# Head softmax on six single score banks, with a later inverse product and the last addition on VectorE

## The chip, the core and the metric

One core of a Trainium2 chip runs the whole kernel. The metric is device microseconds from start to end, as the median of several runs; less is better.

## What is computed

The kernel is a four-layer decoder on a stream of 2 x 512 tokens with 256 features and a context of 2 x 1024 tokens. The change touches one of its attentions, the cross attention of layer 1, whose softmax runs over the 16 heads and not over the keys:

```python
scores = jnp.einsum('bhqd,bhkd->bhqk', mh_q, mh_k) / sqrt(HD)   # 16 heads of 16 features
score = jax.nn.softmax(scores, axis=1)                          # axis 1: the heads
att = jnp.einsum('bhqk,bhkd->bhqd', score, mh_v)
```

So for each pair of a query and a key there is one maximum and one sum over 16 numbers, and nothing is carried from key to key but the product with the values.

## The kernel before

`head_softmax_stage` (tiles named `a1x_...`) computes this attention in 64 tiles: 2 batches, 4 query tiles and 8 key tiles, each of 128 keys (partitions) by 128 queries by 16 heads. The order on every engine is written out by hand, with semaphores between the engines; each engine takes its instructions in order. Tile n goes through these steps:

- **Scores** (TensorE, `score`, L1471): 16 products of 128 columns into `scores`, a ring of three double banks of 8 heads each; a tile fills two. Each half waits until the exponentials have read what stood there three halves before.
- **Maximum** (VectorE, L1530): one reduction over 2048 numbers, where the tile's two double banks lie next to each other. In every third tile they wrap around the ring; then two reductions of 1024 (L1534) go into `most_half`, and a small maximum of the two (L1536) joins them.
- **Shift** (TensorE, `shift`, L1482): four products of 512 columns subtract the maximum from the scores in place.
- **Exponential** (ScalarE, L1551): two of 1024 columns, into one of four buffers of `experts`.
- **Sum over heads** (GpSimd): four additions, of 1024 (L1588), 512 (L1590), 256 (L1592) and 128 columns (L1596, into `total`).
- **Inverse** (ScalarE, `invert`, L1559 and L1564): the logarithm, and the exponential of its negative, into a PSUM bank.
- **Division** (VectorE, `divide`, L1520): one product over 2048 columns, in place.
- **Value product** (TensorE, `value`, L1497): 32 instructions that add over eight key tiles into `u`, which `u_out` on ScalarE (L1570) copies out after the eighth.

The engines interleave tiles. VectorE takes the maximum of tile n and then the division of tile n-2. TensorE takes the first half of the scores of n+1, the shift of n, the second half of the scores of n+1, and the values of n-2. ScalarE takes the exponentials of n and then the inverse of n-1. SyncE loads the second batch's queries, keys and values piece by piece, each piece after a wait on the count of scores or value products that frees its place.

Of the kernel before, what the change touches and what calls it, by code (L numbers as in the profile page):

```python
# [17 lines left out]
P = 128  # L18
# [1356 lines left out]
def head_softmax_stage(core, name, qs, ks, q_parts, k_parts, v_scr, aoT, ex, loads=()):  # L1375
# [12 lines left out]
    HALVES = 2  # L1388
    with stage(core, name) as st:
# [12 lines left out]
        mh = st.sb("most_half", [P, HALVES, P])  # L1402
        tree = st.sb("tree", [P, 8, P])
        tree2 = st.sb("tree2", [P, 4, P])
        tree3 = st.sb("tree3", [P, 2, P])
# [11 lines left out]
        with nc.Block() as block:  # L1417
            @block.sync
            def _(sp):
                def load(b, which, part):  # L1420
                    for dst, src in head_softmax_loads(qs, ks, b, which, part, q_parts, k_parts):
                        sp.dma_start(dst, src).then_inc((q_in, k_in)[which][part], 16)

                def load_values(b, t):
                    sp.dma_start(vs[:, t, :], v_scr[b, t * P:(t + 1) * P].rearrange("t g c -> t (g c)")
                                 ).then_inc(v_in[t], 16)

                load(0, 1, 1)
                core.landed(sp)
                for t in range(4):  # L1430
                    load_values(0, t)
                load(0, 1, 2)
                for t in range(4, 6):
                    load_values(0, t)
                load(0, 1, 3)
                for t in range(6, KT):
                    load_values(0, t)
                load(0, 0, 1)
                prefetch(sp, loads, loaded)
                for b in range(1, B):  # L1440

                    sp.wait_ge(scored, HALVES * (b * UB - 2 * KT))
                    load(b, 0, 0)
                    for quarter in range(4):

                        sp.wait_ge(scored, HALVES * (b * UB - KT + 2 * quarter + 2))
                        load(b, 1, quarter)
                        for t in range(2 * quarter, 2 * quarter + 2):
                            sp.wait_ge(valued, b * UB - KT + t + 1)
                            load_values(b, t)  # L1450
                    load(b, 0, 1)
                end_prefetch(sp, loads, loaded)

            @block.tensor
            def _(pe):
                def score(n, half):
                    b, qt, kt = place(n)
                    if n == 0 and half == 0:
                        pe.wait_ge(core.first_in, core.first_at)
                    if half == 0 and kt == 0 and qt % (QT // 2) == 0 and (b or qt):  # L1460
                        pe.wait_ge(q_in[2 * qt // QT], (b + (qt > 0)) * (16 * len(RUNS)))
                    if half == 0 and qt == 0 and kt % 2 == 0 and (b or kt):
                        pe.wait_ge(k_in[kt // 2], (b + (kt > 0)) * (16 * len(RUNS)))
                    g = HALVES * n + half
                    if g >= 3:

                        pe.wait_ge(expd, g - 2)
                    for i in range(2):
                        for j in range(4):
                            h = 8 * half + 4 * i + j  # L1470
                            mm = nc.tensor.matmul(sp_[:, g % 3, i, j, :], ks[0:96, h, kt * P:(kt + 1) * P],  # L1471
                                                  qs[0:96, h, qt * P:(qt + 1) * P], start=(j == 0), stop=False,
                                                  skip_group_check=True)
                    mm.then_inc(scored, 1)

                def shift(n):

                    pe.wait_ge(most, n + 1)
                    for half in range(HALVES):
                        g = HALVES * n + half  # L1480
                        for i in range(2):
                            mm = nc.tensor.matmul(sp_[:, g % 3, i, :, :], minus[:, :],  # L1482
                                                  mx[:, n % 2, :].unsqueeze(1).to_broadcast([P, 4, P]),
                                                  start=False, stop=True, skip_group_check=True)
                        mm.then_inc(less, 1)
# [17 lines left out]
                for half in range(HALVES):  # L1503
                    score(0, half)
# [12 lines left out]
            def _(dve):  # L1517
# [6 lines left out]
                nc.vector.tensor_scalar(minus[:, :], core.ident_bf[:, :], -1.0, None, ALU.mult).then_inc(minus_in, 1)  # L1524
                for n in range(N):
                    dve.wait_ge(scored, HALVES * (n + 1))
                    g = HALVES * n % 3
                    if g < 2:
                        src = sp_[:, g:g + 2, :, :, :].rearrange("p g i j q -> p q (g i j)")
                        nc.vector.tensor_reduce(mx[:, n % 2, :], src, AX.X, ALU.max).then_inc(most, 1)  # L1530
                    else:
                        for half in range(HALVES):
                            src = sp_[:, (g + half) % 3, :, :, :].rearrange("p i j q -> p q (i j)")
                            nc.vector.tensor_reduce(mh[:, half, :], src, AX.X, ALU.max).then_inc(most_half, 1)  # L1534
                        dve.wait_ge(most_half, HALVES * (n // 3 + 1))
                        nc.vector.tensor_tensor(mx[:, n % 2, :], mh[:, 0, :], mh[:, 1, :], ALU.max).then_inc(most, 1)  # L1536
                    if n >= 2:
                        divide(n - 2)
# [4 lines left out]
            def _(act):  # L1543
                def exp(n):
# [3 lines left out]
                    for half in range(HALVES):  # L1548
                        g = HALVES * n + half
                        act.wait_ge(less, g + 1)  # L1550
                        nc.scalar.activation(ex[:, n % E, 8 * half:8 * half + 8, :],  # L1551
                                             sp_[:, g % 3, :, :, :].rearrange("p i j q -> p (i j) q"), ACT.Exp
# [31 lines left out]
            def _(pool):  # L1584
                for n in range(N):
                    e = ex[:, n % E, :, :]
                    pool.wait_ge(expd, HALVES * (n + 1))
# [2405 lines left out]
```

## Time and profile before

| | |
|---|---|
| time, median of 3 runs | 2276.43 us (2266.73 to 2276.82) |
| span of the profiled execution | 2262.2 us; its own time, which is not listed apart, is one of this kind: the runs lie 4.5 to 14.6 us above this span |
| busy over the whole span | TensorE 81%, VectorE 65%, ScalarE 47%, GpSimd 36% |
| the stage | first score at 704.6 us, end of the last copy at 1052.8 us |

The span runs from the first to the last instruction. An engine's busy time is what the profiler records of its instructions; bracketed in a row of the timeline stands how long the engine sat idle before an instruction, and what released it. Most of the kernel lies outside the stage and is the same before and after the change.

### The profile page before, as it was taken

Reading aid. Unit: us, or ns where it says so; the run is one execution under the profiler, and the core shown is the slowest. Engines: PE = TensorE matmul, PEld = TensorE weight load, DVE = VectorE, ACT = ScalarE, POOL = GpSimd, SP = SyncE. Lnnn points to the kernel's source line nnn. Section 1 sums busy time; section 2 is a strip of 40 time slices with the busy share of each in tenths; the row PEclk is TensorE's granted clock in tenths of the full one; section 3 lists DMA queues with packets and bytes.
Section 4 is the critical chain, followed back from the end, with each engine's and each line's share of the span. In section 5 each row is a group of like instructions: output and inputs, shape, how many; then the busy total and the mean of one; then the engine's idle time right before and its main releaser. Section 6 shows DMA issues by size and latency. Waiting matters only on the chain. (4 is left out here: it accounts for less than half of the span.)

```text
span 2262.2 us, 32189 instructions
## 1 busy us (share of the span) xinstructions
PE 1835.8 (81%) x11356; PEld 920.9 (41%) x11379; DVE 1477.1 (65%) x2550; ACT 1073.0 (47%) x1821; POOL 823.1 (36%) x744
## 2 busy tenths in 40 slices
PE   5888979999875767767797788999879796899954
PEld 3444423333543444445485452333246543122223
DVE  4544266663666998896434547999744555788676
ACT  3453124445333444453344343888834424266746
POOL 1000035554244999995304110666732222000012
PEclk9999989999986898898797899999979897699967
DMA  6612551210029115001514844222035500444000
GB/s 187 161 37 84 190 169 63 66 47 1 19 71 223 24 21 94 2 1 71 190 41 142 190 136 97 69 54 65 20 134 194 166 10 17 104 106 93 20 1 19
DMA packets 174401, 192.08 MB, mean 85 GB/s; under 512 B 15844, under 2 KB 140334, under 8 KB 173334
## 3 DMA queue, kind: packets, MB, share of 16 engines
q1 hardware_dynamic: 171172, 181.64, 29.5%
q0 software_dynamic: 3072, 8.39, 1.2%
q8 instruction: 93, 1.52, 0.3%
q14 instruction: 64, 0.52, 0.1%
HBM read 125.61 MB, written 68.30 MB: 86 GB/s over the span
## 5 line engine op out<-in xcount | busy, mean ns | idle before, releaser
L3461 POOL TENSOR_TENSOR a2x_masked<-a2x_masked,tall_rows 128x512 f32<-128x512 f32 x128 | 163.2, 1276 | 126.3 <-ACT a2x_masked L3423 126.3
L1551 ACT ACTIVATE experts<-a1x_scores 128x1024 f32<-128x1024 f32 x128 | 124.1, 1021 | 163.7 <-PE a1x_scores L1482 163.7
L3472 DVE TENSOR_REDUCE a3x_row_most<-a3x_ring 128x1 f32<-128x512 f32 x256 | 162.9, 684 | 26.0 <-PE a3x_ring L3311 24.9
L3472 DVE TENSOR_REDUCE a2x_row_most<-a2x_ring 128x1 f32<-128x512 f32 x256 | 162.3, 679 | 5.0 <-DMA a2a_qs<-a2a_shift 3.4
L1588 POOL TENSOR_TENSOR a1x_tree<-experts 128x1024 f32<-128x1024 f32 x64 | 150.4, 2350 | 32.9 <-ACT experts L1551 32.4
L671 POOL TENSOR_TENSOR a0x_pair_sums<-a0x_probs_T 128x1024 f32<-128x1024 f32 x48 | 114.8, 2391 | 129.2 <-ACT a0x_probs_T L800 101.8
L854 DVE TENSOR_REDUCE ctx_then_heads<-a0x_rows 128x2 f32<-128x1024 f32 x88 | 107.7, 1224 | 81.7 <-PE a0x_rows L689 81.5
L1520 DVE TENSOR_TENSOR experts<-experts,a1x_inverse_total 128x2048 f32<-128x2048 f32 x64 | 145.7, 2276 | 4.2 <-ACT a1x_inverse_total L1564 4.2
L3416 ACT ACTIVATE a3x_probs_T<-a3x_scores_T 128x1024 f32<-128x1024 f32 x128 | 123.0, 1018 | 46.6 <-PE a3x_scores_T L3338 46.6
L1471 PE MATMUL a1x_scores<-a1x_qs,a1x_ks 96*128 96x128 bf16 x1024 | 93.0, 244 | 59.3 <-ACT experts L1551 45.0
L3416 ACT ACTIVATE wide_rows<-a2x_masked 128x1024 f32<-128x1024 f32 x128 | 135.9, 1062 | 1.4 <-POOL a2x_masked L3461 1.4
L800 ACT ACTIVATE a0x_probs_T<-a0x_scores_T 128x1024 f32<-128x1024 f32 x96 | 98.3, 1024 | 76.6 <-PE a0x_scores_T L715 63.6
L1530 DVE TENSOR_REDUCE a1x_most<-a1x_scores 128x128 bf16<-128x2048 f32 x43 | 98.5, 2291 | 33.2 <-PE a1x_scores L1471 33.2
L1482 PE MATMUL a1x_scores<-a1x_most,a1x_minus_ident 128*128 128x512 bf16 x256 | 71.6, 405 | 56.7 <-DVE a1x_most L1536 32.5
L1471 PEld LDWEIGHTS a1x_scores<-a1x_qs,a1x_ks 96*128 96x128 bf16 x1024 | 69.1, 110 | 108.5 <-ACT experts L1551 78.5
L3311 PE MATMUL a2x_ring<-a2x_ks,a2x_qs 97*128 97x512 bf16 x256 | 99.2, 387 | 8.2 <-DMA a2x_qs<-in_ones_bf 5.2
L3484 DVE TENSOR_TENSOR a2x_masked<-a2x_scores_T,tall_rows 128x512 f32<-128x512 f32 x128 | 87.6, 685 | 22.7 <-ACT wide_rows L3416 13.8
L711 PE MATMUL a0x_scores_T<-ctx_then_heads 64*128 64x512 f32 x384 | 101.6, 607 | 0.7 <-ACT ctx_then_heads L806 0.7
L728 PE MATMUL a0x_u<-a0x_probs_T,a0x_vs 128*64 128x512 f32 x384 | 92.8, 605 | 0.0
L3423 ACT COPY a2x_masked<-a2x_scores_T 128x512 f32<-128x512 f32 x128 | 74.7, 584 | 36.7 <-PE a2x_scores_T L3338 30.5
L1497 PE MATMUL a1x_u<-experts,a1x_vs 128*32 128x128 f32 x2048 | 86.3, 321 | 6.1 <-DVE experts L1520 6.1
L3314 PE MATMUL a2x_ring<-wide_rows,ident_bf 128*128 128x512 bf16 x234 | 90.1, 385 | 0.0
(676 smaller groups left out, 4206.0 us busy)
## 6 DMA issues: line engine op xcount, KB each, us to landing
v_scr<-p0x_vout SPq DMA_DIRECT2D x24, 256.0 KB, 2.0
k_scr<-p0x_x SPq DMA_DIRECT2D x24, 256.0 KB, 2.3
ctx_then_heads<-k_scr SPq DMA_DIRECT2D x8, 768.0 KB
a0x_vs<-v_scr SPq DMA_DIRECT2D x8, 768.0 KB, 4.8
experts<-in_L_ffn_w SPq DMA_DIRECT2D x8, 768.0 KB, 6.7
v_scr<-experts SPq DMA_DIRECT2D x16, 256.0 KB, 2.2
a1x_vs<-v_scr SPq DMA_DIRECT2D x16, 256.0 KB, 5.5
v_scr<-m1f_vout SPq DMA_DIRECT2D x16, 256.0 KB, 2.5
```

The costliest lines, as they stand in the source:

```text
L671: nc.gpsimd.tensor_tensor(pair[:, n // 2 % RP, :, :], pT[:, (n - 1) % R, :, :], pT[:, n % R, :, :], ALU.add).then_inc(paired, 1)
L711: nc.tensor.matmul(sT[:, n % 2, h, :], ks[hs, u % 3, kt * P:(kt + 1) * P], qs[hs, u % 3, :], start=True, stop=False, skip_group_check=True)
L854: nc.vector.tensor_reduce(rm[:, qt, :, c], row_psum(r)[:, :, :], AX.X, ALU.max).then_inc(row_most, 1)
L1471: mm = nc.tensor.matmul(sp_[:, g % 3, i, j, :], ks[0:96, h, kt * P:(kt + 1) * P], qs[0:96, h, qt * P:(qt + 1) * P], start=(j == 0), stop=F ...
L1520: nc.vector.tensor_tensor(ex[:, n % E, :, :], ex[:, n % E, :, :], rp[:, 0, :].unsqueeze(1).to_broadcast([P, H, P]), ALU.mult).then_inc(nor ...
L1530: nc.vector.tensor_reduce(mx[:, n % 2, :], src, AX.X, ALU.max).then_inc(most, 1)
L1551: nc.scalar.activation(ex[:, n % E, 8 * half:8 * half + 8, :], sp_[:, g % 3, :, :, :].rearrange("p i j q -> p (i j) q"), ACT.Exp).then_inc ...
L1588: nc.gpsimd.tensor_tensor(tree[:, :, :], e[:, 0:8], e[:, 8:16], ALU.add).then_inc(folded, 1)
L3311: mm = nc.tensor.matmul(out, lhsT, rhs, start=True, stop=True, skip_group_check=True)
L3416: nc.scalar.activation(pT[:, n % R, 2 * half:2 * half + 2, 0:w], src, ACT.Exp).then_inc(expd, 1)
L3461: nc.gpsimd.tensor_tensor(sm[:, i % 2, 1, :], sm[:, i % 2, 1, :], full[1][:, i // 2 % KT, :], ALU.add).then_inc(pool_masked, 1)
L3472: nc.vector.tensor_reduce(rm[:, u % 2, h * QT + qt:h * QT + qt + 1, part], ring[:, row_place(r) % 3, 0:n], AX.X, ALU.max).then_inc(row_mos ...
```

## The change

The ring of three double banks becomes a ring of six single banks of four heads. Scores, shift and exponentials count banks: four waits and signals a tile where there were two, and four exponentials of 512 columns where there were two of 1024. A bank of new scores waits for the exponential of that bank alone. On VectorE the division comes three tiles behind the maximum and not two; on ScalarE the inverse comes two tiles behind the exponentials and not one; on TensorE the value product comes four tiles behind, and stands ahead of the shift. In the third tile that wraps, the two half reductions each wait for their own two banks. The last of the four additions of the sum over heads (128 columns, into `total`) moves from GpSimd to VectorE, between the maximum and the division; `tree3` gets a second buffer for it.

```diff
-    HALVES = 2
+    BANKS = 4
+    RING = 6
...
-        sp_ = st.ps("scores", [P, 3, 2, 4, P])
+        sp_ = st.ps("scores", [P, RING, 4, P])
...
-                    sp.wait_ge(scored, HALVES * (b * UB - 2 * KT))
+                    sp.wait_ge(scored, BANKS * (b * UB - 2 * KT))
...
+                    g = BANKS * n + i
+                    if g >= RING:
+
+                        pe.wait_ge(expd, g - RING + 1)
+                    for j in range(4):
...
                 for n in range(N):
                     if n + 1 < N:
                         score(n + 1, 0)
+                        score(n + 1, 1)
+                    if n >= 4:
+                        value(n - 4)
                     shift(n)
                     if n + 1 < N:
-                        score(n + 1, 1)
-                    if n >= 2:
-                        value(n - 2)
-                value(N - 2)
-                value(N - 1)
+                        score(n + 1, 2)
+                        score(n + 1, 3)
+                for n in range(N - 4, N):
+                    value(n)
...
+                def most_of(n):
+                    at = BANKS * n % RING
+                    if at + BANKS <= RING:
+                        dve.wait_ge(scored, BANKS * (n + 1))
+                        src = sp_[:, at:at + BANKS, :, :].rearrange("p i j q -> p q (i j)")
+                        nc.vector.tensor_reduce(mx[:, n % 2, :], src, AX.X, ALU.max).then_inc(most, 1)
+                        return
+                    for half, i in enumerate((at, 0)):
+                        dve.wait_ge(scored, BANKS * n + 2 * half + 2)
+                        src = sp_[:, i:i + 2, :, :].rearrange("p i j q -> p q (i j)")
+                        nc.vector.tensor_reduce(mh[:, half, :], src, AX.X, ALU.max).then_inc(most_half, 1)
+                    dve.wait_ge(most_half, 2 * (n // 3 + 1))
+                    nc.vector.tensor_tensor(mx[:, n % 2, :], mh[:, 0, :], mh[:, 1, :], ALU.max).then_inc(most, 1)
+
+                def add_up(n):
+                    dve.wait_ge(folded, 3 * (n + 1))
+                    if n >= 2:
+                        dve.wait_ge(logged, n - 1)
+                    nc.vector.tensor_tensor(tot[:, n % 2], tree3[:, n % 2, 0], tree3[:, n % 2, 1], ALU.add
+                                            ).then_inc(total, 1)
+
                 for n in range(N):
...
+                    most_of(n)
                     if n >= 2:
-                        divide(n - 2)
+                        add_up(n - 2)
+                    if n >= 3:
+                        divide(n - 3)
+                add_up(N - 2)
+                divide(N - 3)
+                add_up(N - 1)
                 divide(N - 2)
                 divide(N - 1)
...
                 for n in range(N):
+                    if n >= KT and n % KT == 3:
+                        u_out(n - 4)
                     exp(n)
-                    if n >= 1:
-                        invert(n - 1)
-                    if n >= KT and n % KT == 1:
-                        u_out(n - 2)
+                    if n >= 2:
+                        invert(n - 2)
+                invert(N - 2)
                 invert(N - 1)
                 u_out(N - 1)
...
-                    nc.gpsimd.tensor_tensor(tree3[:, :, :], tree2[:, 0:2], tree2[:, 2:4], ALU.add).then_inc(folded, 1)
-                    pool.wait_ge(folded, n * 3 + 3)
                     if n >= 2:
-                        pool.wait_ge(logged, n - 1)
-                    nc.gpsimd.tensor_tensor(tot[:, n % 2], tree3[:, 0], tree3[:, 1], ALU.add).then_inc(total, 1)
+                        pool.wait_ge(total, n - 1)
+                    nc.gpsimd.tensor_tensor(tree3[:, n % 2], tree2[:, 0:2], tree2[:, 2:4], ALU.add).then_inc(folded, 1)
```

## Rows read from the trace of the kernel before

**Rows 1.** Windows view, steady stretch: busy us of PE, PEld, DVE, ACT, POOL

```profile
712.00:1040.00 328.00, 228.14 (x3198) 145.57 (x3196) 294.23 (x167) 157.04 (x256) 299.79 (x250) 0.88 0.22 38
```

**Rows 2.** Groups by line, same stretch: busy us, mean ns, idle us before

```profile
L1588 POOL TENSOR_TENSOR a1x_tree<-experts 128x1024 f32<-128x1024 f32 x63 | 148.0, 2350 | 32.9 <-ACT experts L1551 32.4
...
L1520 DVE TENSOR_TENSOR experts<-experts,a1x_inverse_total 128x2048 f32<-128x2048 f32 x62 | 141.1, 2276 | 0.0
...
L1590 POOL TENSOR_TENSOR a1x_tree<-a1x_tree 128x512 f32<-128x512 f32 x63 | 80.3, 1274 | 4.9
...
L1592 POOL TENSOR_TENSOR a1x_tree<-a1x_tree 128x256 f32<-128x256 f32 x62 | 45.1, 728 | 4.9
...
L1596 POOL TENSOR_TENSOR a1x_total<-a1x_tree 128x128 f32<-128x128 f32 x62 | 28.2, 455 | 4.9
```

**Rows 3.** Timeline of one tile's chain: start us, us, engine, line

```profile
861.16 1.94 PE L1497 MATMUL a1x_u<-experts,a1x_vs 128*32 128x128 f32 x32
...
865.99 1.08 PE L1497 MATMUL a1x_u<-experts,a1x_vs 128*32 128x128 f32 x32
...
866.10 2.29 DVE L1530 TENSOR_REDUCE a1x_most<-a1x_scores 128x128 bf16<-128x2048 f32 x1 [0.34 <-PE a1x_scores L1471]
...
868.44 1.04 PE L1482 MATMUL a1x_scores<-a1x_most,a1x_minus_ident 128*128 128x512 bf16 x4 [0.82 <-DVE a1x_most L1530]
...
869.15 1.94 ACT L1551 ACTIVATE experts<-a1x_scores 128x1024 f32<-128x1024 f32 x2 [2.31 <-PE a1x_scores L1482]
...
870.23 1.03 PE L1471 MATMUL a1x_scores<-a1x_qs,a1x_ks 96*128 96x128 bf16 x8 [0.74 <-ACT experts L1551]
...
871.29 2.36 DVE L1534 TENSOR_REDUCE a1x_most_half<-a1x_scores 128x128 f32<-128x1024 f32 x2 [0.71 <-PE a1x_scores L1471]
```

**Rows 4.** Timelines, reduction of the fourth and of the last tile

```profile
724.70 2.29 DVE L1530 TENSOR_REDUCE a1x_most<-a1x_scores 128x128 bf16<-128x2048 f32 x1 [1.09 <-PE a1x_scores L1471]
...
1036.86 2.29 DVE L1530 TENSOR_REDUCE a1x_most<-a1x_scores 128x128 bf16<-128x2048 f32 x1 [0.30 <-PE a1x_scores L1471]
```

**Rows 5.** Other stages, by form and by line: mean ns; ns min/median/max

```profile
L3416 ACT ACTIVATE a0a_probs_T<-a0a_scores_T 128x512 f32<-128x512 f32 x10 | 6.0, 597 | 7.9 <-PE a0a_scores_T L3343 7.9
...
L2427 DVE TENSOR_TENSOR m2f_h<-m2f_silu,m2f_pp x31: 286/288/290, 1719.0 to 1768.2; 128x128 f32<-128x128 f32 x31
```

**Rows 6.** One line's durations, ns min/median/max, first and last start

```profile
L1536 DVE TENSOR_TENSOR a1x_most<-a1x_most_half x21: 292/606/1299, 714.5 to 1028.3; 128x128 bf16<-128x128 f32 x21
```

**Rows 7.** Timeline around one joining maximum, VectorE and GpSimd

```profile
1026.66 2.34 POOL L1588 TENSOR_TENSOR a1x_tree<-experts 128x1024 f32<-128x1024 f32 x1
...
1028.35 0.81 DVE L1536 TENSOR_TENSOR a1x_most<-a1x_most_half 128x128 bf16<-128x128 f32 x1
...
1029.08 2.27 DVE L1520 TENSOR_TENSOR experts<-experts,a1x_inverse_total 128x2048 f32<-128x2048 f32 x1
...
1029.08 1.27 POOL L1590 TENSOR_TENSOR a1x_tree<-a1x_tree 128x512 f32<-128x512 f32 x1
```

**Rows 8.** Timelines elsewhere, pairs starting together; and one line's durations

```profile
523.09 1.22 DVE L883 TENSOR_TENSOR a0x_three_pairs<-a0x_three_pairs,a0x_pair_sums 128x1024 f32<-128x1024 f32 x1
...
523.13 3.39 POOL L671 TENSOR_TENSOR a0x_pair_sums<-a0x_probs_T 128x1024 f32<-128x1024 f32 x1 [3.68 <-DVE a0x_three_pairs L883]
...
621.53 1.27 POOL L1317 TENSOR_TENSOR r1a_kv<-r1a_k,r1a_v 128x512 f32<-128x512 f32 x1 [2.44 <-ACT r1a_v L1288]
...
621.53 1.82 DVE L1362 SCALAR_TENSOR_TENSOR r1a_scan_kv<-r1a_kv,r1a_rate,r1a_scan_kv 128x512 f32<-128x512 f32 x1
...
L1362 DVE SCALAR_TENSOR_TENSOR r1a_scan_kv<-r1a_kv,r1a_rate,r1a_scan_kv x4: 752/1161/1819, 614.7 to 635.3; 128x512 f32<-128x512 f32 x4
```

**Rows 9.** DMA view, one issue group; KB each, median us to landing

```profile
a1x_ks<-k_scr SPq DMA_DIRECT2D x8, 384.0 KB, 6.2
```

**Rows 10.** Timeline, the stage's last division

```profile
1047.87 2.29 DVE L1520 TENSOR_TENSOR experts<-experts,a1x_inverse_total 128x2048 f32<-128x2048 f32 x1 [2.71 <-ACT a1x_inverse_total L1564]
```

More of the change, by code:

```diff
@@ L1440, in _ @@
                 for b in range(1, B):
-                    sp.wait_ge(scored, HALVES * (b * UB - 2 * KT))
+                    sp.wait_ge(scored, BANKS * (b * UB - 2 * KT))
                     load(b, 0, 0)
                     for quarter in range(4):
-                        sp.wait_ge(scored, HALVES * (b * UB - KT + 2 * quarter + 2))
+                        sp.wait_ge(scored, BANKS * (b * UB - KT + 2 * quarter + 2))
                         load(b, 1, quarter)
@@ L1455, in _, with score @@
             def _(pe):
-                def score(n, half):
+                def score(n, i):
                     b, qt, kt = place(n)
-                    if n == 0 and half == 0:
+                    if n == 0 and i == 0:
                         pe.wait_ge(core.first_in, core.first_at)
-                    if half == 0 and kt == 0 and qt % (QT // 2) == 0 and (b or qt):
+                    if i == 0 and kt == 0 and qt % (QT // 2) == 0 and (b or qt):
                         pe.wait_ge(q_in[2 * qt // QT], (b + (qt > 0)) * (16 * len(RUNS)))
-                    if half == 0 and qt == 0 and kt % 2 == 0 and (b or kt):
+                    if i == 0 and qt == 0 and kt % 2 == 0 and (b or kt):
                         pe.wait_ge(k_in[kt // 2], (b + (kt > 0)) * (16 * len(RUNS)))
[L1464 to L1473, printed above, removed]
+                    g = BANKS * n + i
+                    if g >= RING:
+                        pe.wait_ge(expd, g - RING + 1)
+                    for j in range(4):
+                        h = 4 * i + j
+                        mm = nc.tensor.matmul(sp_[:, g % RING, j, :], ks[0:96, h, kt * P:(kt + 1) * P],
+                                              qs[0:96, h, qt * P:(qt + 1) * P], start=(j == 0), stop=False,
+                                              skip_group_check=True)
                     mm.then_inc(scored, 1)
@@ L1478, in shift @@
                     pe.wait_ge(most, n + 1)
[L1479 to L1485, printed above, removed]
+                    for i in range(BANKS):
+                        nc.tensor.matmul(sp_[:, (BANKS * n + i) % RING, :, :], minus[:, :],
+                                         mx[:, n % 2, :].unsqueeze(1).to_broadcast([P, 4, P]),
+                                         start=False, stop=True, skip_group_check=True).then_inc(less, 1)
                 def value(n):
@@ L1502, in _ @@
                 pe.wait_ge(minus_in, 1)
-                for half in range(HALVES):
-                    score(0, half)
+                for i in range(BANKS):
+                    score(0, i)
                 for n in range(N):
@@ L1547, in exp @@
                         act.wait_ge(valued, n - E + 1)
-                    for half in range(HALVES):
-                        g = HALVES * n + half
+                    for i in range(BANKS):
+                        g = BANKS * n + i
                         act.wait_ge(less, g + 1)
-                        nc.scalar.activation(ex[:, n % E, 8 * half:8 * half + 8, :],
-                                             sp_[:, g % 3, :, :, :].rearrange("p i j q -> p (i j) q"), ACT.Exp
+                        nc.scalar.activation(ex[:, n % E, 4 * i:4 * i + 4, :], sp_[:, g % RING, :, :], ACT.Exp
                                              ).then_inc(expd, 1)
@@ L1586, in _ @@
                     e = ex[:, n % E, :, :]
-                    pool.wait_ge(expd, HALVES * (n + 1))
+                    pool.wait_ge(expd, BANKS * (n + 1))
                     nc.gpsimd.tensor_tensor(tree[:, :, :], e[:, 0:8], e[:, 8:16], ALU.add).then_inc(folded, 1)
```

15 lines of the change are left out of this document (2 added, 13 removed).

## The prediction

> **What bounds the stage now.** I read the window of the steady stretch first, then the groups by line, then the timeline of single tiles. The window [rows 1] shows no engine full: of 328 us VectorE is busy 294.2, GpSimd 299.8, TensorE 228.1, ScalarE 157.0. From the fourth to the last reduction, 60 tiles, pass 312.16 us [rows 4]: 5.203 us a tile, 15.6 us for three (three, because every third tile wraps around the ring).
>
> The timeline [rows 3] shows the loop that sets this pace. A reduction ends at 868.39 (866.10 + 2.29); the shift starts 0.05 later; the first exponential at 869.15, 0.76 after the maximum; its half of the ring is free about 1.02 later; then eight score products (870.23, 1.03 us at TensorE's lower clock) must end before the next reduction starts at 871.29. VectorE stood idle 0.71 us there, and the bracket names the scores as releaser. GpSimd is close behind: its four additions take 2.35 + 1.27 + 0.73 + 0.455 = 4.81 us a tile [rows 2], with 0.08 us between them.
>
> The reader should see one more thing, off this loop. The joining maximum L1536 has 128 columns, and its durations run from 0.29 to 1.30 us, median 0.61 [rows 6]. In [rows 7] it starts at 1028.35 and ends at 1029.16; GpSimd's addition of 1024 columns, running since 1026.66, ends at 1029.00. This row stands for 21: in each of them L1536 ends 0.14 to 0.25 us after a GpSimd addition's end. The division (one operand in SBUF, one in PSUM) runs beside the same additions and always takes 2.28 [rows 2]. So a VectorE instruction with two SBUF operands waits until the GpSimd addition in flight is over.
>
> The Trainium skill (SBUF — State Buffer, "Who interferes with whom") states this as a rule: a VectorE instruction with two inputs in SBUF and a GpSimd instruction that reads SBUF exclude each other for the whole instruction, and the one that starts first goes first. By that rule L1536 would wait as it does; the trace agrees, 0.81 us in [rows 7] where 0.29 is the least.
>
> **The change, part by part.** I write M for the end of a tile's maximum.
>
> *The ring of single banks.* The first exponential needs one shift product and not two. Four take 1.04, so a quarter of that is saved: M + 0.5. An exponential of 512 columns takes 0.60 [rows 5]; two of 1024 (1.02 each) take 1.94 together [rows 3], so each starts 0.10 before the last one's end. The second ends at M + 1.6, the fourth at M + 2.6 (now M + 2.70: 869.15 + 1.94 - 868.39). The last bank of the next tile's scores waits for the second, and takes half of the 0.6 to 1.0 us of eight products: the next maximum may start at M + 2.0 to 2.2, where it now starts 2.90 after (871.29 - 868.39). The four exponentials cost ScalarE 0.2 us a tile more, hidden: it is busy 48% of the window.
>
> *What VectorE then does between two maxima.* A division, 2.28, less the 0.08 by which each instruction starts ahead of its forerunner's end (1029.08 against 1029.16 in [rows 7]). That is 2.2, and with the added addition more: longer than the new loop. So the loop no longer decides; VectorE does.
>
> *The division three tiles behind, the values four behind.* The division waited 0.0 us for the inverse [rows 2], so the longer lag takes nothing off. Value products ahead of the shift take 1.08 at the full clock, 1.94 at half [rows 3]; they end by M + 4.2 or 5.3, against a next maximum at 4.6 or later. I count nothing at the full clock; at half, where the cover is short, up to 0.5 us a tile. SyncE's waits on the value count come two tiles later, about 10 us, but four tiles (20 us) stay ahead of the first use of a key piece, which lands in 6.2 [rows 9]; the pieces queued behind them on SyncE have the same slack. `u_out` ahead of the exponentials is hidden while the values end before the next maximum. The doubled semaphore signals I count as nothing: the steps from one engine's end to the next one's start in [rows 3] are 0.03 to 0.1 us with their signals in them, and their number along the loop stays the same.
>
> *The last addition.* GpSimd loses 0.455 + 0.08 a tile. VectorE gains an instruction of 128 columns with both operands in SBUF: by its size 0.29 [rows 5], 0.21 net of overlap; but it is of the kind of L1536. Lower bound 0.21; upper bound, a wait for a whole 1.27 or 2.35 addition. Which one is decided by where GpSimd stands when the maximum ends.
>
> *The walk through three tiles.* GpSimd's 1024 addition starts 0.1 after the exponentials, M + 2.7, and ends M + 5.05; its 512 addition runs from 5.13 to 6.40. Take a wrapping tile with M = 0, its joining maximum freed by a 1024 addition that ended at -0.15. The 512 addition starts at -0.07 and runs to 1.20. The added addition would start at -0.08. Both are ready within 0.01 us. [Rows 7] show just this: the division, next on VectorE, and the 512 addition both start at 1029.08. If GpSimd goes first, the addition ends at 1.20 + 0.15 = 1.35; division to 3.55; maximum to 5.76. The next addition arrives at 5.68, inside the 512 addition that lasts to 6.40, and ends at 6.55; division to 8.75, maximum to 10.96. The third arrives at 10.88, once more on the start of a 512 addition (10.89). Won, the next joining maximum ends at 16.2; lost, at 17.5. So three tiles take 16.2 to 17.5 against 15.6: a loss of 0.6 to 1.9, over 21 triples 12 to 40 us. I take the middle, 26.
>
> *Who goes first?* [Rows 8]: a VectorE addition that started 0.04 before a GpSimd one went first, and the GpSimd one took 3.39 (an undisturbed one of that size takes 2.35 [rows 2]). Where both started at 621.53, GpSimd took its undisturbed 1.27 and VectorE 1.82, its least being 0.75. A tie went to GpSimd; I take that.
>
> *The tail.* After the last maximum (ends 1039.15) the last division now ends at 1050.16 [rows 4, 10], 11.0 later. Then: last GpSimd addition M + 7.1, added addition 7.4, but the division of tile 62 is queued behind it, to 9.6, and that of 63 ends at 11.8: +1.
>
> **Sum.** 26 + 1 = +27 us. Against the profiled span of 2262.2 us that is 2289; the runs lie 4.5 to 14.6 above that span, the median 14.2, so I add to the median: 2276.4 + 27 = **2303**. A change of 0.5% (11.4 us) is about what a measurement of this kernel can tell from none.
>
> **Rivals.**
>
> *VectorE goes first after the joining maximum.* Then the addition ends at 0.21 and nothing of it is lost; maximum to 4.62. The next addition arrives at 4.54, waits for the end of the 1024 addition at 5.05, ends at 5.20; maximum to 9.61; the third ends at 9.82, and the next joining maximum at 14.8. Gain 0.8 a triple, 17 us, less 1 for the tail and some 4 to 5 where TensorE runs at half clock (granted 0.88 in the window, so about a quarter of the time, some 15 tiles at 0.3): -12, 2264. For it: VectorE is ready 0.01 earlier. Against: the tie at 621.53. It turns on a start of 0.01 us; from there everything is on the other side of no change.
>
> The Trainium skill's rule in the same section, the first to start goes first, would give this rival's 2264 if the profile's start is the moment that counts, and the forecast if GpSimd's claim comes first; [rows 8] agree with the rule at 0.04 us and cannot tell at 0.01.
>
> *The addition meets no wait at all* (its phase falls into GpSimd's gaps, or the wait does not hold for it): VectorE needs 4.62 twice and 5.0 once, 14.2 a triple, -29 us, +1, +4 for the clock: 2252. Against it: 21 of 21 cases of L1536 waited or came at the end of an addition.
>
> *The change does nothing that can be measured*: the order after the joining maximum alternates, and tiles of both kinds cancel: 2276, or within 11.4 of it. For it: a stretch at the lower clock moves GpSimd against VectorE and can flip the order.
>
> **Chances.** Forecast 0.53, VectorE first 0.28, no wait 0.06, cancelling 0.13. VectorE first lies astride -0.5%, half on either side. So faster 0.06 + 0.14 = 0.20, same 0.14 + 0.13 = 0.27, slower 0.53. The forecast's own range is 2289 to 2317. The range for 8 in 10 must take in most of VectorE first: 2260 to 2316 leaves out no wait (0.06), the low end of VectorE first (0.05) and the top of the forecast (0.06).
>
> **What would show it.** Right: VectorE's instruction that writes `total` takes 0.8 to 1.4 us in most tiles, and ends 0.15 us after the end of a GpSimd addition, often the 512 one; VectorE is hardly ever idle ahead of a maximum; three tiles take 16.2 to 17.5 us from maximum to maximum. Ring: the first score bank lands well before VectorE takes it up, and the exponentials end at M + 2.6. Wrong: additions of 0.29 to 0.7 and three tiles in 15 us or less (VectorE goes first), or all of 0.29 (no wait). A division that waits for its inverse, or a key piece that TensorE waits for in the second batch, would upset the parts I counted as nothing.

## The result, and the profile after

The changed kernel takes 2253.90 us (median of 7 runs), the kernel before 2269.11 (median of 7): ratio 0.9928, interval 0.9904 to 0.9952 (the two medians by themselves give 0.9933). So the change makes the kernel faster by 0.7%, 16 us, where I had forecast a loss of 27 us. The measured median lies below the range, too.

The gain shows in the stage that was changed. From the end of the first tile's maximum to that of the 64th, the kernel before takes 330.36 us (708.79 to 1039.15) and the changed one 316.85 (712.74 to 1029.59), 13.5 less. The profiled execution of the changed kernel was the slowest of its seven runs (2262.05), so its span is no measure of the whole; inside the stage it can be read tile by tile. The two profiled spans differ by 2.1 us only (2262.2 and 2260.1), although the stage, from its first score to its last copy, takes 336.3 and not 348.2: the rest of the kernel, which the change leaves alone, took 1914 us in the one and 1924 in the other, and lies between 1912 and 1929 over all twelve profiles of this document. So the whole is compared by medians of several runs, and the stage within a profile.

First the windows view of the kernel after: the steady stretch, as [rows 1], and 80 us out of its middle (busy us of PE, PEld, DVE, ACT, POOL; granted clock; DMA share; GB/s).

```profile
712.00:1030.00 318.00, 235.40 (x3174) 133.28 (x3175) 310.01 (x229) 163.10 (x381) 275.19 (x188) 0.95 0.23 42
825.00:905.00 80.00, 58.56 (x850) 32.63 (x840) 79.79 (x61) 41.80 (x98) 71.47 (x49) 1.00 0.46 77
```

VectorE is now the bound: 310.0 of 318 us, and 79.8 of 80 in the middle, where it was busy 294 of 328. GpSimd fell from 299.8 of 328 us (91%) to 275.2 of 318 (87%), and TensorE's granted clock rose from 0.88 to 0.95, to 1.00 in the middle. The groups by line of the same stretch, by form, answer to [rows 2] (busy us, mean ns, idle us before, and what ended it):

```profile
L1603 POOL TENSOR_TENSOR a1x_tree<-experts 128x1024 f32<-128x1024 f32 x63 | 148.2, 2353 | 48.3 <-ACT experts L1566 47.1
L1519 DVE TENSOR_TENSOR experts<-experts,a1x_inverse_total 128x2048 f32<-128x2048 f32 x61 | 138.7, 2274 | 0.0
L1566 ACT ACTIVATE experts<-a1x_scores 128x512 f32<-128x512 f32 x252 | 130.1, 602 | 147.4 <-PE a1x_scores L1480 147.4
...
L1529 DVE TENSOR_REDUCE a1x_most<-a1x_scores 128x128 bf16<-128x2048 f32 x43 | 98.0, 2279 | 13.1 <-PE a1x_scores L1471 12.9
...
L1605 POOL TENSOR_TENSOR a1x_tree<-a1x_tree 128x512 f32<-128x512 f32 x63 | 82.5, 1310 | 4.9
...
L1542 DVE TENSOR_TENSOR a1x_total<-a1x_tree 128x128 f32<-128x128 f32 x62 | 28.9, 465 | 0.0
```

The reductions waited 43.8 us for scores before, in all 64 tiles (33.2 at L1530, 10.6 at L1534); 14.6 are left, in six tiles (12.9 at L1529, 1.7 at L1534): 13.8 of it in the first four tiles of the stage, and twice 0.44 near 767 and 783. GpSimd now stands idle 48.3 us ahead of its first addition, nearly all of it for exponentials, where it stood 32.9. The added instruction, L1542, costs 28.9 us, 465 ns each on the mean.

How the 465 ns are made up shows in the timeline of the middle, one triple from joining maximum to joining maximum, VectorE and GpSimd:

```profile
868.40 2.35 POOL L1603 TENSOR_TENSOR a1x_tree<-experts 128x1024 f32<-128x1024 f32 x1 [0.48 <-ACT experts L1566]
...
870.41 0.49 DVE L1536 TENSOR_TENSOR a1x_most<-a1x_most_half 128x128 bf16<-128x128 f32 x1
870.82 0.28 DVE L1542 TENSOR_TENSOR a1x_total<-a1x_tree 128x128 f32<-128x128 f32 x1
870.83 1.41 POOL L1605 TENSOR_TENSOR a1x_tree<-a1x_tree 128x512 f32<-128x512 f32 x1
...
871.03 2.27 DVE L1519 TENSOR_TENSOR experts<-experts,a1x_inverse_total 128x2048 f32<-128x2048 f32 x1
873.22 2.28 DVE L1529 TENSOR_REDUCE a1x_most<-a1x_scores 128x128 bf16<-128x2048 f32 x1
875.42 0.67 DVE L1542 TENSOR_TENSOR a1x_total<-a1x_tree 128x128 f32<-128x128 f32 x1
...
880.41 0.28 DVE L1542 TENSOR_TENSOR a1x_total<-a1x_tree 128x128 f32<-128x128 f32 x1
```

This is the moment that decided the forecast. The joining maximum ends (870.41 + 0.49), freed by the 1024-column addition that ended at 870.75. The added addition starts at 870.82, the 512-column addition at 870.83, and it is GpSimd's that grows: 1.41 instead of 1.27, while VectorE's takes 0.28. In the second tile the added addition waits for the end of the 1024-column one (0.67); in the third it starts 0.14 us before such an addition ends and loses nothing (0.28). Maxima end 4.60, 4.99 and 5.19 us apart, over and over: 14.78 us for three tiles. That is the rival "VectorE goes first", with its 14.8.

Once, outside of a disturbed stretch that is told of below, the order falls the other way:

```profile
986.61 2.35 POOL L1603 TENSOR_TENSOR a1x_tree<-experts 128x1024 f32<-128x1024 f32 x1 [0.47 <-ACT experts L1566]
988.62 0.49 DVE L1536 TENSOR_TENSOR a1x_most<-a1x_most_half 128x128 bf16<-128x128 f32 x1
989.04 1.27 POOL L1605 TENSOR_TENSOR a1x_tree<-a1x_tree 128x512 f32<-128x512 f32 x1
989.05 1.40 DVE L1542 TENSOR_TENSOR a1x_total<-a1x_tree 128x128 f32<-128x128 f32 x1
```

GpSimd starts at 989.04, VectorE at 989.05: now the 512-column addition keeps its 1.27 and VectorE's takes 1.40. The next three steps from maximum to maximum are 5.74, 5.19 and 5.19, 16.12 in all: the forecast's own triple (16.2), one out of 21. The second profile of this kernel shows the same, in the same tile (1.40).

### The profile page after: what moved, and what is told of

It reads as the page before. It is cut to its first block and busy times, and to the rows that moved or that the text cites. A ratio compares the mean times of both kernels' runs of the same rounds, so it can differ in the third digit from the quotient of the medians.

```text
span 2260.1 us, 32379 instructions
## 1 busy us (share of the span) xinstructions
PE 1844.8 (82%) x11356; PEld 910.0 (40%) x11379; DVE 1496.1 (66%) x2614; ACT 1078.6 (48%) x1949; POOL 798.4 (35%) x680
## 5 line engine op out<-in xcount | busy, mean ns | idle before, releaser
L1566 ACT ACTIVATE experts<-a1x_scores 128x512 f32<-128x512 f32 x256 | 132.2, 602 | 149.9 <-PE a1x_scores L1480 149.9
L1471 PE MATMUL a1x_scores<-a1x_qs,a1x_ks 96*128 96x128 bf16 x1024 | 104.3, 233 | 35.2 <-DMA a1x_ks<-k_scr 14.2
L1529 DVE TENSOR_REDUCE a1x_most<-a1x_scores 128x128 bf16<-128x2048 f32 x43 | 98.0, 2279 | 13.1 <-PE a1x_scores L1471 12.9
L1471 PEld LDWEIGHTS a1x_scores<-a1x_qs,a1x_ks 96*128 96x128 bf16 x1024 | 64.3, 104 | 96.0 <-ACT experts L1566 77.0
L3496 DVE TENSOR_TENSOR a2x_masked<-a2x_scores_T,tall_rows 128x512 f32<-128x512 f32 x128 | 87.7, 685 | 22.7 <-ACT wide_rows L3428 13.8
L1605 POOL TENSOR_TENSOR a1x_tree<-a1x_tree 128x512 f32<-128x512 f32 x64 | 83.8, 1310 | 5.0
```

What stands on the lines that cost most here:

```text
L1471: mm = nc.tensor.matmul(sp_[:, g % RING, j, :], ks[0:96, h, kt * P:(kt + 1) * P], qs[0:96, h, qt * P:(qt + 1) * P], start=(j == 0), stop=F ...
L1566: nc.scalar.activation(ex[:, n % E, 4 * i:4 * i + 4, :], sp_[:, g % RING, :, :], ACT.Exp).then_inc(expd, 1)
```

## The experiments

The theory after the result: the ring takes the scores off the path and leaves VectorE as the bound; the addition can then leave GpSimd at little cost, because at the joining maximum VectorE's addition comes a hair ahead of GpSimd's. The rivals: the order doesn't matter and the ring alone gives the gain; the addition's move alone gives it; the longer lags give it. Where the quoted expectations speak of theory A, it is the first.

**A step that should delay the addition.** A write of one column ahead of the added addition, in every third tile, and behind it as a control.

```diff
+        nudge = st.sb("nudge", [P, 1])
...
+                    if n % 3 == 1:
+                        nc.vector.memset(nudge[:, :], 0.0)
                     if n >= 2:
                         add_up(n - 2)
```

> The changed kernel with a one-column VectorE write put between the joining maximum and the added addition in every third tile (21 small instructions, some 0.07 us each by the step between short VectorE instructions). Theory A (the addition is cheap only because it is ready 0.01 us ahead of GpSimd's 512 addition): GpSimd now goes first, these additions last 1.2 to 1.4 us and not 0.28, three tiles take 16.2 to 17.5 us and not 14.8, and the kernel is 15 to 50 us slower than the changed one, ratio to before 1.000 to 1.015. Rival B (VectorE keeps its turn when one instruction follows the other closely): three tiles 14.8 to 14.9 us, 21 times 0.07 = 1.5 us, ratio 0.993.

> The same one-column write in the same tiles, but behind the added addition and ahead of the division: the control of the first. Theory A and rival B agree: three tiles 14.8 to 14.9 us, ratio 0.993 to 0.994. If it is as slow as the first, the small write costs something of its own and the first tells nothing.

Measured: 2257.23 us ahead (before 2267.45), ratio 0.9941 [0.9911, 0.9971]; behind 2254.55, 0.9942 [0.9905, 0.9979]. The expected loss did not come, and the timeline of the first one says why:

```profile
825.58 0.28 DVE L1543 TENSOR_TENSOR a1x_total<-a1x_tree 128x128 f32<-128x128 f32 x1
825.60 0.06 DVE L1549 MEMSET a1x_nudge<- 128x1 f32 x1
825.78 2.27 DVE L1520 TENSOR_TENSOR experts<-experts,a1x_inverse_total 128x2048 f32<-128x2048 f32 x1
...
825.58 1.42 POOL L1608 TENSOR_TENSOR a1x_tree<-a1x_tree 128x512 f32<-128x512 f32 x1
```

The write is recorded inside the addition, and the addition starts 0.42 after the joining maximum's start (825.16), as without it. So there was no delay worth the name, and the run decides nothing. It did move the start by some nanoseconds: both rows say 825.58 (read to the nanosecond, VectorE starts 1 to 3 behind GpSimd in 20 of the 21 tiles; in the changed kernel it was 3 to 9 ahead), and VectorE still goes first.

**A delay that is one.** A reduction of 64 columns of the maximum's own halves, ahead of and behind the added addition, in every third tile. The amount of work is the same in both kernels. The lines stand against the kernel with the write ahead.

```diff
                     if n % 3 == 1:
-                        nc.vector.memset(nudge[:, :], 0.0)
+                        nc.vector.tensor_reduce(nudge[:, :], mh[:, 0, 0:64].unsqueeze(1), AX.X, ALU.max)
```

> The one-column write of the first run took no time of VectorE (the added addition still started with GpSimd's 512 addition), so here a reduction of 64 columns stands between the joining maximum and the added addition in every third tile: some 0.14 us. Theory A (a tie within 0.01 us that VectorE wins): GpSimd goes first, these 21 additions last about 1.3 us and not 0.28, three tiles take 16.2 to 17.5 us, ratio to before 1.00 to 1.02. Rival B (VectorE keeps its turn): additions of 0.28, three tiles 14.9 to 15.0, ratio 0.993 to 0.995.

> Control: the same reduction of 64 columns in the same tiles, but behind the added addition and ahead of the division. Theory A and rival B agree: additions of 0.28 there, three tiles 14.9 to 15.0 us, ratio 0.993 to 0.996.

Measured: ahead 2282.04 us (before 2269.11), 1.0046 [1.0016, 1.0077]; behind 2255.43, 0.9938 [0.9909, 0.9967]. The same instruction, moved by one place, is worth 1.1%. The kernel with the delay ahead:

```profile
880.00 0.49 DVE L1537 TENSOR_TENSOR a1x_most<-a1x_most_half 128x128 bf16<-128x128 f32 x1
880.41 0.21 DVE L1549 TENSOR_REDUCE a1x_nudge<-a1x_most_half 128x1 f32<-128x64 f32 x1
880.54 1.29 DVE L1543 TENSOR_TENSOR a1x_total<-a1x_tree 128x128 f32<-128x128 f32 x1
...
886.15 0.86 DVE L1543 TENSOR_TENSOR a1x_total<-a1x_tree 128x128 f32<-128x128 f32 x1
...
880.42 1.27 POOL L1608 TENSOR_TENSOR a1x_tree<-a1x_tree 128x512 f32<-128x512 f32 x1
```

The addition starts 0.12 behind the 512-column one, takes 1.29 and ends 0.14 after it; the second takes 0.86, the third 0.28. Maxima end 5.75, 5.18 and 5.19 apart. The forecast's walk had 5.76, 5.20 and 5.2: had GpSimd gone first, the walk with a won third (16.2) would have been right to 0.1 us, and the kernel slower than before, by 0.5%. The 16.12 lie just under the 16.2 to 17.5 expected for this run. With the delay behind, the same rows read 0.28, 0.54, 0.40 for the three additions:

```profile
876.02 0.37 DVE L1537 TENSOR_TENSOR a1x_most<-a1x_most_half 128x128 bf16<-128x128 f32 x1
876.31 0.28 DVE L1543 TENSOR_TENSOR a1x_total<-a1x_tree 128x128 f32<-128x128 f32 x1
876.51 0.20 DVE L1551 TENSOR_REDUCE a1x_nudge<-a1x_most_half 128x1 f32<-128x64 f32 x1
```

**The ring without the addition's move.** First ring, lags and order kept, the last addition back on GpSimd; then the old lags as well, so that only the ring and the bank-by-bank exponentials are left.

```diff
+                    nc.gpsimd.tensor_tensor(tree3[:, 0], tree2[:, 0:2], tree2[:, 2:4], ALU.add).then_inc(folded, 1)
+                    pool.wait_ge(folded, n * 3 + 3)
...
-                    nc.gpsimd.tensor_tensor(tree3[:, n % 2], tree2[:, 0:2], tree2[:, 2:4], ALU.add).then_inc(folded, 1)
...
+                    nc.gpsimd.tensor_tensor(tot[:, n % 2], tree3[:, 0, 0], tree3[:, 0, 1], ALU.add).then_inc(total, 1)
```

```diff
-                    if n >= 3:
-                        divide(n - 3)
+                        divide(n - 2)
...
-                    if n >= 4:
-                        value(n - 4)
+                    if n >= 2:
+                        value(n - 2)
```

> The changed kernel with the last addition put back on GpSimd: ring of single banks and all lags stay. Theory A has GpSimd's chain of 2.35 + 1.27 + 0.73 + 0.455 plus four steps of 0.08 = 5.1 us a tile become the bound: 15.2 to 15.5 us for three tiles against 15.6 before, a gain of 2 to 8 us, ratio 0.996 to 0.999. Rival C (ring and lags alone bring the gain, the place of the addition does not matter): ratio 0.993 or less.

> Of the change only the ring of six single banks with the exponentials bank by bank; the old lags (division two tiles behind, inverse one, values two and behind the scores) and all four additions on GpSimd. Theory: GpSimd's chain of 5.1 us a tile decides as in the run with the addition back on GpSimd, and the lags do nothing: 15.2 to 15.5 us for three tiles, ratio 0.996 to 0.999. Rival C' (the lags carry part of the gain): 15.6 or more, ratio 1.000 or above.

Measured: 2262.93 us, 0.9966 [0.9939, 0.9994], and 2261.85, 0.9975 [0.9940, 1.0011]. Both as expected: about 0.3%, though the second's interval takes in no change at all. In both profiles three tiles take 15.3 us (15.35 and 15.33), about a third of the way from before (15.61) to after (14.78). The timeline of the first shows what GpSimd costs there:

```profile
861.22 2.35 DVE L1534 TENSOR_REDUCE a1x_most_half<-a1x_scores 128x128 f32<-128x1024 f32 x2
863.60 1.87 DVE L1536 TENSOR_TENSOR a1x_most<-a1x_most_half 128x128 bf16<-128x128 f32 x1
...
862.99 2.34 POOL L1592 TENSOR_TENSOR a1x_tree<-experts 128x1024 f32<-128x1024 f32 x1
...
868.16 2.36 POOL L1592 TENSOR_TENSOR a1x_tree<-experts 128x1024 f32<-128x1024 f32 x1
873.39 2.35 POOL L1592 TENSOR_TENSOR a1x_tree<-experts 128x1024 f32<-128x1024 f32 x1 [0.18 <-ACT experts L1555]
...
878.39 2.35 POOL L1592 TENSOR_TENSOR a1x_tree<-experts 128x1024 f32<-128x1024 f32 x1
```

GpSimd stands idle once in these three tiles (0.18 before 873.39), and its rounds take 15.40 (862.99 to 878.39): its chain of about 5.1 us a tile is the bound, as expected. With its four additions GpSimd comes later, its 1024-column addition starts (862.99) inside the halves' reductions and ends at 865.33, and the joining maximum stands there for 1.87 us (1.1 to 1.9 over the 21 tiles). The second kernel takes back the longer lags as well, with the places of the steps around them: with the addition on GpSimd they carry nothing that can be measured.

**The addition's move without the ring.** The kernel before with the last addition on VectorE behind the division.

```diff
+                    if n >= 1:
+                        add_up(n - 1)
...
-                    nc.gpsimd.tensor_tensor(tot[:, n % 2], tree3[:, 0], tree3[:, 1], ALU.add).then_inc(total, 1)
```

> The kernel before with only the last addition moved to VectorE (behind the division, one tile behind the maximum, so that the old lag of the inverse holds): old ring of three double banks, two exponentials a tile. Theory: GpSimd is freed (4.6 us a tile), but the old loop from one maximum to the next (the next one starts 2.6 to 2.9 us after) still decides, and the addition, which waits for GpSimd up to that point, adds nothing or up to 0.3 us a tile: 15.4 to 16.2 us for three tiles, ratio 0.998 to 1.006. Rival: the addition's move alone is the gain, ratio 0.994 or less.

Measured: 2263.31 us (before 2269.66), 0.9972 [0.9946, 0.9997]; 15.44 us for three tiles. The tiles came as expected, the ratio fell just under the expected range. All 64 additions take 0.28 to 0.29, because they come into GpSimd's gaps, and GpSimd's tree is sometimes late for them (idle 0.33 in the row). The joining maximum, too, waits less: 0.29 to 0.39 in 19 of the 21 tiles, where the median was 0.61 [rows 6].

```profile
873.09 0.29 DVE L1528 TENSOR_TENSOR a1x_total<-a1x_tree 128x128 f32<-128x128 f32 x1 [0.33 <-POOL a1x_tree L1604]
873.30 2.28 DVE L1537 TENSOR_REDUCE a1x_most<-a1x_scores 128x128 bf16<-128x2048 f32 x1
```

**The addition behind the division**, in the changed kernel, and the changed kernel once more beside it.

```diff
-                    if n >= 2:
-                        add_up(n - 2)
                     if n >= 3:
                         divide(n - 3)
+                    if n >= 2:
+                        add_up(n - 2)
```

> The changed kernel with the added addition behind the division and not ahead of it, in every tile. Theory A by the same walk: in plain tiles the addition arrives 2.1 us after the maximum, inside GpSimd's 256 addition, and waits to its end (0.4 to 0.8 us); in the wrapping tile GpSimd is idle and it takes 0.28; three tiles 14.6 to 15.0 us without any tie, ratio 0.991 to 0.994. If the place ahead of the division is what makes the addition cheap, it is 15.2 us or more and the ratio above 0.996.

> The changed kernel once more, beside the run with the addition alone: steady pattern of three tiles 14.8 us (additions of 0.28, 0.67, 0.28), and a ratio of 0.992 to 0.995. If the stretches with additions of 1.3 us, which the first profile showed at its beginning, come after a drop of TensorE's clock, they lie elsewhere or are missing here.

Measured: 2251.86 us, 0.9915 [0.9881, 0.9950], 14.78 us for three tiles; the changed kernel again 2257.42, 0.9952 [0.9914, 0.9990]. Two in three additions then take 0.28, the third 0.63 (expected was the reverse, a wait in both plain tiles), and the two places can't be told apart by these runs. So the place ahead of the division is not what makes the addition cheap: behind it no addition comes within 0.02 us of the start of a GpSimd one, and three tiles take the same 14.78.

**No wait at all.** The addition and the joining maximum as reductions over one operand of 256 columns, which leaves the work the same and takes away the second operand.

```diff
-                    nc.vector.tensor_tensor(mx[:, n % 2, :], mh[:, 0, :], mh[:, 1, :], ALU.max).then_inc(most, 1)
+                    nc.vector.tensor_reduce(mx[:, n % 2, :], mh[:, :, :].rearrange("p h q -> p q h"), AX.X, ALU.max).then_inc(most, 1)
...
-                    nc.vector.tensor_tensor(tot[:, n % 2], tree3[:, n % 2, 0], tree3[:, n % 2, 1], ALU.add
+                    nc.vector.tensor_reduce(tot[:, n % 2], tree3[:, n % 2].rearrange("p i q -> p q i"), AX.X, ALU.add
```

> The changed kernel with the added addition and the joining maximum written as reductions over one operand of 256 columns in place of an operation on two operands of 128. If the wait belongs to two operands in SBUF, both stop waiting: 0.34 us each always (256 columns at the pace of the 2048 that take 2.28, plus 0.07), no duration near 0.5 to 1.4; three tiles 14.3 to 14.5 us against 14.8, another 6 to 9 us off the stage, ratio 0.988 to 0.991. If the wait hangs on something else (any short VectorE instruction beside GpSimd), durations stay spread and the ratio is 0.993 or worse.

Measured: 2251.13 us, 0.9911 [0.9885, 0.9937], the lowest median of all, though not told apart from the change itself. All 64 additions take 0.41 to 0.43, wherever GpSimd stands:

```profile
866.20 0.42 DVE L1536 TENSOR_REDUCE a1x_most<-a1x_most_half 128x128 bf16<-128x256 f32 x1
866.54 0.41 DVE L1542 TENSOR_REDUCE a1x_total<-a1x_tree 128x128 f32<-128x256 f32 x1
866.87 2.28 DVE L1519 TENSOR_TENSOR experts<-experts,a1x_inverse_total 128x2048 f32<-128x2048 f32 x1
...
864.06 2.35 POOL L1603 TENSOR_TENSOR a1x_tree<-experts 128x1024 f32<-128x1024 f32 x1 [0.22 <-ACT experts L1566]
866.50 1.27 POOL L1605 TENSOR_TENSOR a1x_tree<-a1x_tree 128x512 f32<-128x512 f32 x1
```

The joining maximum runs to its end at 866.62 across the end of one GpSimd addition (866.41) and the start of the next, and the added one runs beside a 512-column addition that keeps its 1.27. The division in the third row is a TENSOR_TENSOR as the addition was, but has one of its two operands in PSUM; beside the same 512-column addition it keeps its 2.28. So the wait belonged to two operands in SBUF, and not to short instructions or to this operation as such. I had expected 0.34 for the addition and 14.3 to 14.5 us for three tiles; at 0.41 they take 14.73, as much as with the waits (14.78). What the wait costs, the larger form costs too. What it may be worth is that the time no longer hangs on who comes first: this profile shows no disturbed tile, and 308.65 us from the first to the last maximum, 8.2 less than the profiled change.

## Why the prediction was wrong

**The failed step.** "A tie went to GpSimd; I take that." Behind the joining maximum VectorE's addition went first, by less than 0.01 us, and took 0.28; GpSimd's grew to 1.41, and three tiles took 14.78 us in place of 16.2 to 17.5. The row that the step rests on, 621.53 in [rows 8], is of another instruction, and no precedent for this one. In the second profile of the changed kernel the same pair stands 0.02 apart, VectorE ahead, and VectorE waits all the same:

```profile
621.60 1.84 DVE L1362 SCALAR_TENSOR_TENSOR r1a_scan_kv<-r1a_kv,r1a_rate,r1a_scan_kv 128x512 f32<-128x512 f32 x1
621.62 1.27 POOL L1317 TENSOR_TENSOR r1a_kv<-r1a_k,r1a_v 128x512 f32<-128x512 f32 x1 [2.46 <-ACT r1a_v L1288]
```

In all twelve profiles these two start within 0.02 us of each other, and VectorE waits every time (1.80 to 1.84), first or second. For the addition of 128 columns the recorded start decides: ahead by 0.01, it wins (870.82), behind by 0.01, it loses (989.05). Over the seven profiles of the new ring with this addition of two operands on VectorE, it went first in all 106 cases in which it started from 0.02 us ahead of a GpSimd addition to 0.003 behind, and waited in all 33 in which it started 0.009 to 0.2 behind. The nearer reading was the one that the prediction put second: the order of the starts in [rows 7] themselves, worked out as 0.01 in favour of VectorE. Those rows print 1029.08 twice; read to the nanosecond, VectorE is ahead there, 1029.077 against 1029.082. Which part of the two instructions makes the difference to 621.53 was not tried.

The Trainium skill (SBUF — State Buffer, "Who interferes with whom") says that the instruction that issues first goes first. If the recorded start stands for the issue, the traces agree for the addition, to better than a hundredth of a microsecond, and disagree at 621.60.

**The walk itself was right**, on both sides: 4.62, 4.99, 5.19 worked out for VectorE first, 4.60, 4.99, 5.19 measured; 5.76, 5.20, 5.2 for GpSimd first, 5.75, 5.18, 5.19 measured with the delay ahead. The forecast took the middle of won and lost thirds (+26); with GpSimd first nearly all thirds are won (0.28), and three tiles take 16.15 on the mean: 0.5 more than before, 11 us over 21 triples. So even with GpSimd first the forecast's +27 was about twice too large: the kernel with the delay ahead is 13 us slower than before.

**Sizes.** The sum stood on a median of three runs, 2276.4; the median of seven is 2269.1, so 7 of the 10 us between the rival's 2264 and the measured 2253.9 lie in that base. Told as differences, the rival had 12 less than before; measured were 15 to 16 less. Its 0.8 a triple held: in an execution without disturbed tiles (the kernel with the column's write ahead) the last 20 triples take 295.6 us and not 312.2, 0.83 less each, and the first three steps give another 2.5 (15.7, not 18.2). The term of this sum that was mis-sized is TensorE at half clock (4 to 5 us): in that execution it costs nothing. Of 64 tiles' value products, 20 took over 1.5 us before, 7 after. In the kernel before, a pause ahead of the shift is followed by products at half clock (start, us, and the idle time before in brackets):

```profile
776.08 0.62 PE L1471 MATMUL a1x_scores<-a1x_qs,a1x_ks 96*128 96x128 bf16 x8 [0.74 <-ACT experts L1551]
...
779.99 1.04 PE L1482 MATMUL a1x_scores<-a1x_most,a1x_minus_ident 128*128 128x512 bf16 x4 [1.73 <-DVE a1x_most L1536]
781.77 1.03 PE L1471 MATMUL a1x_scores<-a1x_qs,a1x_ks 96*128 96x128 bf16 x8 [0.74 <-ACT experts L1551]
```

Eight products take 0.62 at 776.08 and 1.03 at 781.77, behind idle stretches of 1.73 and 0.74. After the change the longest regular one is shorter, and in the middle the granted clock stays at 1.00:

```profile
870.96 1.04 PE L1480 MATMUL a1x_scores<-a1x_most,a1x_minus_ident 128*128 128x512 bf16 x4 [1.17 <-DVE a1x_most L1536]
872.10 1.86 PE L1471 MATMUL a1x_scores<-a1x_qs,a1x_ks 96*128 96x128 bf16 x16
873.89 1.08 PE L1494 MATMUL a1x_u<-experts,a1x_vs 128*32 128x128 f32 x32
```

Sixteen score products in 1.86 and 32 value products in 1.08. But a pause of that length was once followed by half clock, too:

```profile
747.80 1.04 PE L1480 MATMUL a1x_scores<-a1x_most,a1x_minus_ident 128*128 128x512 bf16 x4 [1.17 <-DVE a1x_most L1536]
748.94 2.07 PE L1471 MATMUL a1x_scores<-a1x_qs,a1x_ks 96*128 96x128 bf16 x16
750.94 1.94 PE L1494 MATMUL a1x_u<-experts,a1x_vs 128*32 128x128 f32 x32
```

So the clock is higher with the new order (0.95 against 0.88 over the steady stretch), but that the shorter pause is the cause is not shown. I had carried over the share of the kernel before. With 311.3 us from first to last maximum in that execution without disturbed tiles the stage gives 19 us up to the last maximum; the profiled change gave 13.5. Less 1.6 for the tail that is 12 to 17.5, and the runs' 16 (11 to 22 by the interval) lie there.

**What lies between** are the one lost tie at 989.05 (1.3 us) and a few triples near 755 to 800, which begin behind value products at half clock (1.94 at 750.94). GpSimd's next addition then comes later against VectorE, and the joining maximum meets the 512-column one:

```profile
757.29 0.86 DVE L1542 TENSOR_TENSOR a1x_total<-a1x_tree 128x128 f32<-128x128 f32 x1
...
762.64 1.32 DVE L1536 TENSOR_TENSOR a1x_most<-a1x_most_half 128x128 bf16<-128x128 f32 x1
```

The two kernels with the column's write do the same work and show the difference: the one with the write ahead keeps a granted clock of 1.00 from 738 to 1027 and has no disturbed triple; the one with it behind has 0.89 between 783 and 903, steps of up to 6.6, and 322.3 us from first to last maximum against 311.3. Without the second operand (reductions of 256 columns) three value products at half clock, 1.93 to 1.94 at 913.9, 958.2 and 1002.6, cost 0.2 us each (steps of 4.91 and not 4.72). So half clock costs little by itself, and much where it shifts the two engines against each other; not every stretch does. What drops the clock, and whether a disturbed triple brings on the next drop, the rows don't show; it stays open, as does how often such a stretch comes in runs that were not profiled.

**The rest held.** The scores are no longer waited for in the steady part; the division waited 0.0 us for its inverse; the later waits of the key pieces hold up nothing in the steady part; the tail from the last maximum to the stage's last instruction grew from 13.65 to 15.2 us, +1.6 for the +1 worked out. VectorE became the bound, as said. "The order alternates, and tiles cancel" came for one triple in 21 outside the disturbed stretch.

**Where the gain comes from.** The ring alone gives 0.25%, with the lags 0.34%; the addition's move alone 0.28%; both together 0.72%, and 0.48% when measured again. The intervals overlap, so that no more than this can be said: either part alone is about a third to a half of it, and the sum agrees with the whole within the intervals. No run has the ring and the moved addition with the old lags; that the lags carry nothing is shown only with the addition on GpSimd. With the addition ahead of the division the gain hangs on the start order at the joining maximum: 0.13 us later there, and the same kernel is 0.46% slower than before. Behind the division that tie does not come up, and the gain is the same.

## What to carry to other kernels

Where two engines lock each other out and the walk ends in a tie, work the time out for both orders and forecast neither with much weight on a precedent; if one is used, it must be of the same operation, and its starts read to the last digit that the trace holds. Where such a tie decides 1%, make the order certain: put the short instruction elsewhere or give it one operand, and compare medians of several runs. When a change moves the bound, take neither the clock nor the idle pattern of the old order into the new sum.

## What the runs showed of the hardware that was not expected

- The order of two additions that lock each other out turns within 0.02 us of their recorded starts: 870.82 against 870.83 VectorE goes first, 989.05 against 989.04 GpSimd does; over seven profiles the turn lies between 0.003 and 0.009 us behind GpSimd's start (106 and 33 cases, none the other way). VectorE pays 1.12 us when it loses (0.28 becomes 1.40), GpSimd only 0.14 (1.27 becomes 1.41).
- For a SCALAR_TENSOR_TENSOR of 512 columns a lead of 0.02 us was not enough (621.60 against 621.62, 1.84 us where 0.75 is the least).
- A write of one column on VectorE (0.06) cost nothing that the timeline shows; a reduction of 64 columns put the next start off by 0.13.
- A reduction over one operand of 256 columns took 0.41 to 0.43 beside any GpSimd addition; an addition of two operands of 128 columns takes 0.28 undisturbed and up to 1.40 behind one, the joining maximum of the same size up to 1.88 (with all four additions on GpSimd).
- Three stretches at half clock cost 0.2 us each where VectorE's short instructions had one operand; with two operands and the same ring such stretches were followed by steps of up to 6.6 us in place of 4.6 to 5.2.
